# Dividing the seven rotating PSUM banks of an attention stage: three for maxima and four for exponentials, in place of four and three

## What is computed

```python
Q, K, V = (jax.nn.relu(x @ W + b) for W, b in ((Wq, bq), (Wk, bk), (Wv, bv)))   # B=8, T=512, H=16, dh=8
scores = jnp.einsum('bqhd,bkhd->bhqk', Qh, Kh) / np.sqrt(dh)
scores = jnp.where(key_mask[:, None, None, :] == 0, NEG, scores)
scores = jnp.where(tril[None, None, :, :] == 0, NEG, scores)
attn = jax.nn.softmax(scores, axis=-1)
attn = attn * query_mask[:, None, :, None]
out = jnp.einsum('bhqk,bkhd->bqhd', attn, Vh).reshape(B, T, U) + x
normalized = (out - mean) / jnp.sqrt(var + EPS)      # then gamma, beta
# whole block: x + attention(xn) * silu(ffn(xn))
```

## Time and profile before

| | us |
|---|---|
| median of the runs | 432.4 |
| the profiled execution | 433.92 |
| its span, first to last instruction | 432.2 |
| PE busy | 371.8 (86%) |
| DVE busy | 364.4 (84%) |
| ACT busy | 288.2 (67%) |
| POOL busy | 205.1 (47%) |
| mean granted TensorE clock | 0.98 of full speed |

### The profile page before, as it was taken

How to read it: one execution, slowest core, us unless ns; L and a number is a source line. 1 busy time by engine, 2 the same in 40 slices (tenths; PEclk the granted TensorE clock), 3 DMA queues, 4 the chain that set the end, 5 groups by cost and what they waited for, 6 DMA issues and landing times.

```text
span 432.2 us, 9673 instructions
## 1 busy us (share of the span) xinstructions
PE 371.8 (86%) x3499; PEld 244.1 (56%) x3499; DVE 364.4 (84%) x846; ACT 288.2 (67%) x572; POOL 205.1 (47%) x525
## 2 busy tenths in 40 slices
PE   0046998999989989999999999999999999999960
PEld 0013676877677764566666566566566566666420
DVE  5989999999795129998999999998998989989417
ACT  0103686898878851777778788678787778778750
POOL 8532274737632032212356465374473565565592
PEclk9999899999999999999999999999999999999995
DMA  7940003564544421256533422523323233240001
GB/s 210 314 116 1 0 2 103 137 142 135 157 112 132 116 72 45 69 127 146 140 110 91 130 72 73 128 59 104 97 70 109 82 99 102 71 106 28 3 0 49
DMA packets 32407, 41.71 MB, mean 97 GB/s; under 512 B 6136, under 2 KB 24936, under 8 KB 32360
## 3 DMA queue, kind: packets, MB, share of 16 engines
q1 hardware_dynamic: 32200, 41.08, 35.1%
q0 software_dynamic: 160, 0.03, 0.0%
HBM read 26.43 MB, written 11.02 MB: 87 GB/s over the span
## 4 chain that ended last, share of the span: by engine, by line
PE 46%; DVE 13%; issue 2%; ACT 1%; POOL 1%; DVEq 0%; ACTq 0%; POOLq 0%
PE banks L1261 16%; PE banks L1244 9%; DVE mx L1059 8%; PE banks L1224 8%; PE banks L1226 6%; PE banks L1246 5%; DVE stats L1104 2%; PE banks L1271 2%; DVE res L1098 1%; ACT pt L1179 1%; PE banks L1233 0%; DVE res L1085 0%; DVE res L1088 0%; DVE mixed L1089 0%; DVE aggr L1108 0%
## 5 line engine op out<-in xcount | busy, mean ns | idle before, releaser
L1059 DVE TENSOR_REDUCE mx<-banks 128x1 f32<-128x512 f32 (+3 forms) x352 | 200.1, 633 | 16.7 <-PE banks L1226 15.0
L1179 ACT ACTIVATE pt<-banks 128x512 f32<-128x512 f32 x320 | 169.3, 601 | 43.7 <-PE banks L1246 36.2
L1261 PE MATMUL banks<-pt,vg 128*18 128x512 f32 (+3 forms) x1024 | 81.4, 436 | 0.7 <-ACT pt L1179 0.7
L948 POOL TENSOR_SCALAR mneg<-mx 128x16 f32<-128x16 f32 x32 | 8.1, 253 | 108.2 <-DVE mx L1059 107.0
L1224 PE MATMUL banks<-k_own,q_own 76*128 76x384 bf16 (+2 forms) x192 | 48.4, 274 | 3.3 <-DVE mx L1059 2.7
L1224 PE MATMUL banks<-w_room 76*128 76x384 bf16 (+2 forms) x192 | 48.1, 274 | 3.3 <-DVE mx L1059 3.3
L1261 PEld LDWEIGHTS banks<-pt,vg 128*18 128x18 f32 x1024 | 23.7, 97 | 43.8 <-issue 33.4
L1244 PE MATMUL banks<-w_room 76*128 76x384 bf16 (+2 forms) x192 | 47.5, 275 | 0.9 <-ACT pt L1179 0.5
L1244 PE MATMUL banks<-q_own,k_own 76*128 76x384 bf16 (+2 forms) x192 | 47.8, 274 | 0.0
L1226 PE MATMUL banks<-k_own,q_own 124*128 124x128 bf16 x256 | 44.0, 219 | 0.0
L1226 PE MATMUL banks<-w_room 124*128 124x128 bf16 x256 | 43.8, 219 | 0.0
(11 more groups left out here) (199 smaller groups left out, 736.4 us busy)
## 6 DMA issues: line engine op xcount, KB each, us to landing
k_scratch<-parts SPq DMA_DIRECT2D x40, 128.0 KB, 2.3
k_own<-k_scratch SPq DMA_DIRECT2D x48, 96.0 KB
w_room<-k_scratch SPq DMA_DIRECT2D x48, 96.0 KB
q_scratch<-parts SPq DMA_DIRECT2D x24, 128.0 KB, 2.3
q_own<-q_scratch SPq DMA_DIRECT2D x32, 96.0 KB
w_room<-q_scratch SPq DMA_DIRECT2D x32, 96.0 KB
w_room<-in_w_dram SPq DMA_DIRECT2D x1, 2048.0 KB, 12.5
q_own<-q_scratch SPq DMA_DIRECT2D x16, 112.0 KB
```

The source lines that it names most:

```text
L1059: dve.tensor_reduce(mx[:, u % 2, heads[0]:heads[-1] + 1, q], banks[:, S0 + slots[0] % SLOTS, 0:w * len(heads)].rearrange("p (h k) -> p h k ...
L1179: act.activation(pt[:, T * j:T * j + T], banks[:, bank(), :], ACT.Exp, scale=SCALE).then_inc(exp_done, 1)
L1261: ins = mm(banks[32 * h:32 * h + VP, OT, P * k:T], vg[:, g, k, h, :], pt[:, KPLACE[k, h]:KPLACE[k, h] + n], start=(k == 0 and g % 2 == 0), ...
```

## The change

The two numbers that divide the seven rotating banks are exchanged. All banks, both initial semaphore values and all waits are worked out from them; the order of instructions on every engine stays what it is. Banks 0 to 2 serve score chunks and outputs, banks 3 to 6 key chunks and maxima, and bank 7 the values as before. The spare matmuls of L1333 write bank 6 before and after.

```diff
-    SLOTS, RING = 4, 3
+    SLOTS, RING = 3, 4
     S0, ST0, OT = 0, SLOTS, SLOTS + RING
```

## The result

The changed kernel takes 438.48 us (median of four runs, 437.7 to 439.71), the kernel before 432.6; the ratio is 1.0133 with a 95% interval of 1.0096 to 1.017. A later comparison on another chip gave 438.01 against 433.18, 1.0117 (1.0097 to 1.0137). The change makes the kernel about 1.2% slower.

The account below looks back on a forecast made before the run. PE and DVE were taken to lead in turn, so only delays of a pass's leader count. Part one's 5.6 us less part two's 0.6 made 5.0 on the 432.4 median: 437.4 us, range 435.0 to 441.0.

Parts of the forecast that it names:

- Part one: Score chunks wait for the third bank use before them, not the fourth: 5.6 us lost in all.
- the six sets: Units 6 to 29, in sets of four passes: each set grows by 0.80 us, together 4.8 us.
- passes 0 and 2: Passes before the sets: pass 2 loses 0.37 us at S.9 without cover, pass 0 is taken to lose 0.45.
- part two: Key chunks wait for the fourth use back: nothing in full passes; last two units gain 1.0 us, 0.6 arriving.
- Pass 6: PE's stretch from K.0 of unit 6 to K.0 of unit 7: S.9 waits for the outputs' bank, 0.80 us lost.
- pass 9: DVE leads; S.7 to S.9 wait for reductions, S.9 0.47 us later, covered with 0.04 us left.
- pass 8: S.9 waits for the outputs' bank, 0.37 us later, covered by DVE's L1098 with 0.25 us slack left.
- Pass 7: No outputs or statistics; third use back free to within 0.02 us at every score chunk: costed at nothing.
- More lost: Rival: covers of passes 8 and 9 both fail, 5.0 us more, 442.4 us in all (439 to 443); chance 0.15.
- Absorbed: Rival: DVE's idle 1.27 us per set takes up the loss, 432 to 434.5 us; chance 0.08.
- Exponentials as the narrow side: Rival: PE's weight loads' 10.1 us of waits for ACT are lost time, fourth bank brings 422.3 us; chance 0.04.
- The clock: Rival: more, shorter PE pauses lower the granted clock, once per set giving about 449 us; chance 0.03.

Follow-up runs that it names:

- own bank: Three score banks, three for key chunks and maxima, bank 6 for the output transposes alone, against the kernel before: 435.22 us, ratio 1.0045.
- fair partner: The kernel before (four and three banks) with L1098 waiting only for the reads of the outputs: 431.58 us against 433.29, ratio 0.9965.
- three and three banks: Three banks for score chunks, three for key chunks and maxima, bank 6 empty: 439.6 us, 1.6 slower than the changed kernel.
- a kernel with a longer wait: The kernel before (four and three banks) with DVE's L1098 moved from behind S.9 of pass 8 to behind S.10: 442.57 us.
- the same move: The kernel before (four and three banks) with DVE's statistics spread over later units for all batches but the last: 433.71 us, ratio 1.0011.

## Why the prediction was right

**The sum.** 5.0 us were predicted; the attention stage grew by 5.3 in the profiles, the medians by 5.9 and 4.8 in two comparisons. The measured 438.48 and 438.01 us lie 1.1 and 0.6 above the 437.4 and within the range. The parts were less exact than the sum. Part one came to 6.0 us on PE, where 5.6 were predicted: the six sets gave 4.7 for 4.8, and passes 0 and 2 what I gave them, but passes 4 and 5, the first with statistics, took 0.43 us more, and they stood in no term. Of this, 0.13 were made good by part two (0.73 for 0.6). A sum right to 0.3 us is in part luck.

**Pass 6**, 0.80 us a set: 0.79 measured, and DVE's idle time before S.10 is 1.03 us where I gave 1.05. The wait for the outputs' bank sets the time of S.9, as predicted. But it makes only 0.35 of the delay; the rest is the 0.47 by which PE enters late from pass 9, which I had called covered but for 0.06. It is covered only as long as the wait for the outputs stands behind it. Without that wait (own bank, against its fair partner) the set still loses 0.49. Pass 6 itself grew by 0.36 and pass 9 by 0.09, pass 8 by 0.35: on PE the loss is spread over three passes, of which DVE's lead in pass 9 takes up part.

**Pass 7**: 0.01 us. **Pass 8**: S.9 comes 0.35 us late and DVE does not notice; without L1098 behind S.9 the set loses 1.20 and not 0.79. The cover is shown. **Pass 9**: the cover of 0.04 us held, since DVE's chain from 233.29 to 249.62 is 16.33 us long where it was 16.37.

**Passes 0 and 2**: 0.34 us for pass 2, as worked out (0.37). For pass 0 I gave 0.45 and nothing for the chunks of units 0 and 1. The sum is right and the place is wrong: from S.0 of unit 0 to K.0 of unit 0 the kernel takes 0.66 us longer, and pass 0 then takes 0.20 less. PE is stopped there at S.0 of unit 2, ahead of K.0, but not by a bank, for the third use back was read at 171.57 us:

```profile
171.91 0.34 PE L1224 MATMUL banks<-k_own,q_own 76*128 76x384 bf16 x1 [0.27 <-DMA q_own<-mT]
```

It waits for the store of unit 0's maxima. Their transpose stands in PE's queue behind S.5 of unit 1, and with three banks that chunk comes one reduction later: the transpose starts 8.80 us after the first score chunk where it started 8.21 after it. In both kernels S.0 of unit 2 follows the issue of the store by 2.3 us. The prediction put these chunks at nothing because DVE limits them, and had not looked at what else stands behind their waits.

**Part two**: nothing in full passes, shown by three and three banks (0.02 us a pass). In the last two units I gave 1.0 us and said that 0.6 arrive because the store of batch 6 holds the end. 1.4 us came, and 0.7 arrived. The step that failed is the reason for what was lost: the store landed at 430.05 us, and L1085 started at 430.75, 0.03 us after the chain of small instructions in front of it, not within 0.3 of the landing. Before, too, these two stood 0.85 us apart in the prediction's own rows. What took the time was L1098, slower by 0.69 us beside POOL. The row for that, 2.50 us in the last batch against 1.14 in full passes, stood in the trace before, and I had not compared them.

**The rivals.** More lost: no, both covers held. Absorbed: no; DVE's idle time grew. Exponentials as the narrow side: no; the weight loads' 10.1 us were hidden, and the fourth bank is worth 0.02 us a pass. The clock: not in the changed kernel's attention, in either profile; but it did fall in a kernel with a longer wait, at 1.6 us for each fall, so 0.03 was little for this rival.

## What to carry to other kernels

When banks are divided between two consumers, find in the trace, for each wait of the producer, when the use one fewer back was released: here the slow read of the outputs, which shares the rotation, makes two passes of a set longer, and the reductions of pass 9 let PE go 0.47 us later; the same shift was worth 0.02 us a pass on the other side. Two delays of one chain do not simply add, so taking away the one that shows (the outputs) can bring out the other. A delay counts only on the engine that leads at that moment, so ask of each who leads there and what covers it. Work moved to where an engine has slack pays only if the engine that contends with it is quiet: the same move gave nothing with POOL beside it and, with POOL replanned and two smaller edits, 1.6%.

## What the runs showed of the hardware

- DVE's L1098 (four instructions, two tensors in SBUF each) takes 1.14 us alone, 2.14 to 3.22 beside POOL's tensor operations. The loss sits in single instructions: 1.34 to 1.42 us in place of 0.34, each ending 0.15 us after the POOL instruction that it met. POOL's small ones go from 0.20 to 0.72 us. Reductions from PSUM do not change.
- PE starts 0.05 to 0.06 us after the end of the instruction that frees its bank, for both ACT and DVE, where PE stands waiting for it.
- Two neighbouring DVE instructions, the second of which waits for the first's end, stand 0.11 us apart; where it need not wait they overlap by 0.09. That was worth 0.2 us a set, 0.35% of the kernel.
- While there was work for PE, the granted clock fell in the attention of one kernel only, three times, to one half (1.2 of 2.4 GHz), the first time after PE had been busy for 3.5 of 4.6 us, at about 1.6 us each. The first stage has up to two falls, in some executions and not in others; with two it is 0.6 to 1.7 us longer than with one or none.
